# A cross-attention and FFN kernel: VectorE's second router placed ahead of a running sum and a pair of reductions, and the guard of the router's sum written to PSUM

## The reference

```python
h = norm(q) ; ig, fg = gates(h, ctx, ctx)
csum = cumsum(log_sigmoid(fg))               # running sum over the tokens, per head
log_D = csum_i - csum_j + ig_j  (j <= i) ;  D = exp(log_D - max_j log_D)
C = (q k^T / 8 + q . rpe[hops]) * D
x = x + headnorm((C / (max(|sum C|, exp(-max)) + 1e-6)) @ v)

xf = norm(x) ; probs = softmax(xf @ gate_w.T)        # 8 experts + 2 null
weights, selected = top_k(probs, 2)
tw = weights * (selected < 8)
denom = tw.sum() ; denom = where(denom > 0, denom, 1)
out = x + base(xf) + base_b + 2 * sum_e (tw/denom)_e * B_e (A_e xf)
```

## Time and profile before

| | |
|---|---|
| median of 3 runs | 3359.31 us (3355.43 to 3362.64) |
| the profiled execution's own time | 3363.58 us |
| its span, first to last instruction | 3361.5 us |
| PE busy | 2958.6 us (88%) |
| DVE busy | 2447.4 us (73%) |
| POOL busy | 2006.5 us (60%) |
| ACT busy | 1944.9 us (58%) |
| first `gate_stats` of a full round, and the last | 1463.69 and 3243.66 us, 29 rounds apart |

### The profile page before, as it was taken

The page is one execution under the profiler, slowest core; times in us unless marked ns, Lnnn a source line. Parts: engine busy times, 40 slices in busy tenths (PEclk is TensorE's granted clock), DMA queues, the critical chain, the costliest instruction groups (busy, mean ns, idle before and its releaser), DMA issues.

```text
span 3361.5 us, 69962 instructions
## 1 busy us (share of the span) xinstructions
PE 2958.6 (88%) x24660; PEld 1856.5 (55%) x24660; DVE 2447.4 (73%) x5100; ACT 1944.9 (58%) x4654; POOL 2006.5 (60%) x2195
## 2 busy tenths in 40 slices
PE   6778777787777776799999999999999999999997
PEld 4555455454444444465666566656656566566564
DVE  5655555555555555688888888888888888888875
ACT  3444444444444443576666666766666667667663
POOL 6777777777777775254454554544545545545453
PEclk8888889989999999799999999999999999999999
DMA  8999999999999998665565565655655555556551
GB/s 277 346 346 350 320 350 347 341 349 345 348 342 349 347 348 303 183 184 174 166 186 174 173 186 177 182 177 167 185 171 175 182 179 172 178 171 188 173 149 58
DMA packets 413325, 799.98 MB, mean 238 GB/s; under 512 B 107290, under 2 KB 211738, under 8 KB 410932
## 3 DMA queue, kind: packets, MB, share of 16 engines
q1 hardware_dynamic: 311988, 453.61, 43.0%
q0 software_dynamic: 82560, 270.60, 24.0%
q10 hardware_dynamic: 18432, 71.31, 5.5%
HBM read 618.02 MB, written 176.69 MB: 236 GB/s over the span
## 4 chain that ended last, share of the span: by engine, by line
PE 36%; POOL 21%; DMA 14%; issue 14%; DVE 11%; ACT 3%; SPq 0%; POOLq 0%; DVEq 0%; ACTq 0%
DMA arena<-in_L_xattn_rpe_dram,arena 14%; PE psum L1752 8%; POOL arena L784 7%; PE psum L1580 6%; PE psum L1596 4%; PE psum L1669 3%; PE psum L1704 3%; PE psum L1681 3%; POOL arena L827 3%; PE psum L1607 3%; PE psum L1756 2%; POOL arena L817 2%; POOL arena L822 2%; POOL arena L838 2%; POOL arena L771 2%
## 5 line engine op out<-in xcount | busy, mean ns | idle before, releaser
L784 POOL DMA_INDIRECT arena<-in_L_xattn_rpe_dram,arena x768 | 734.0, 956 | 239.5 <-issue 182.4
L1580 PE MATMUL psum<-arena 128*128 128x128 f32 x4128 | 615.4, 297 | 194.5 <-DMA arena<-in_L_xattn_rpe_dram,arena 183.1
L1580 PEld LDWEIGHTS psum<-arena 128*128 128x128 f32 x4128 | 488.7, 151 | 430.6 <-DMA arena<-in_L_xattn_rpe_dram,arena 299.6
L981 ACT ACTIVATE arena<-arena 128x512 f32<-128x512 f32 (+3 forms) x1024 | 496.4, 555 | 42.1 <-PE psum L1704 39.2
L1752 PE MATMUL psum<-arena 128*128 128x512 f32 x1024 | 496.5, 597 | 6.1 <-DVE arena L1377 5.9
L1327 DVE TENSOR_TENSOR arena<-psum,arena 128x1024 f32<-128x1024 f32 (+1 forms) x384 | 386.9, 1043 | 135.7 <-PE psum L1681 126.4
L809 POOL TENSOR_SCALAR_AFFINE_SELECT arena<-arena 128x256 f32<-128x256 f32 x256 | 129.7, 507 | 525.7 <-ACT arena L981 524.7
L563 DVE COPY arena<-psum 128x512 f32<-128x512 f32 x384 | 263.7, 689 | 245.8 <-PE psum L1580 242.2
L572 DVE COPY arena<-psum 128x416 f32<-128x416 f32 (+15 forms) x512 | 225.2, 442 | 278.6 <-PE psum L1596 272.5
L1596 PE MATMUL psum<-arena 64*32 64x416 f32 (+7 forms) x8192 | 364.1, 424 | 57.3 <-ACT arena L895 36.8
L563 ACT COPY arena<-psum 128x512 f32<-128x512 f32 x384 | 225.8, 588 | 257.0 <-PE psum L1580 254.5
(11 more groups left out here) (112 smaller groups left out, 4643.0 us busy)
## 6 DMA issues: line engine op xcount, KB each, us to landing
arena<-in_x_dram SPq DMA_DIRECT2D x256, 256.0 KB, 4.3
arena<-gate_rows SPq DMA_DIRECT2D x128, 512.0 KB, 4.4
arena<-in_x_dram SPq DMA_DIRECT2D x512, 64.0 KB
arena<-in_ctx_dram SPq DMA_DIRECT2D x32, 1024.0 KB, 6.6
out_dram<-arena SPq DMA_DIRECT2D x128, 256.0 KB, 2.1
arena<-in_L_xattn_rpe_dram,arena POOLq DMA_INDIRECT x1032
arena<-hop_products SPq DMA_DIRECT2D x128, 128.0 KB, 2.6
arena<-hop_products SPq DMA_DIRECT2D x128, 120.0 KB, 2.5
```

What stands on the lines that cost most here:

```text
L784: nc.gpsimd.indirect_dma_start(out=rows[set_of(n, v)][:, t, :], out_offset=None, in_=rpe[:, :], in_offset=bass.IndirectOffsetOnAxis(ap=her ...
L981: last = nc.scalar.activation(decay[u % DECAYS][:, e, at:at + width], top_pair[p % 2][:, e * S + j * P:e * S + j * P + width], ACT.Exp, bi ...
L1580: last = nc.tensor.transpose(turn_bank(o)[:, q * P:(q + 1) * P], own[:, q * P:(q + 1) * P], ident)
```

## The change

Two things. First, in the FFN's tiles 0 and 1 three steps of DVE are put in another order. Before: `two_weights(3)`, `layer(rf, 2)`, `gates_2`, `pair_sums(ra, 1)`, `output(rf, 0)`, `router(rf, 1)`, `two_weights(4)`. Now: `two_weights(3)`, `output(rf, 0)`, `layer(rf, 2)`, `router(rf, 1)`, `gates_2`, `pair_sums(ra, 1)`, `two_weights(4)`. Second, the guard in all four routers becomes a `tensor_scalar`, whose one tensor is `den` and whose second scalar is the same column, and its result goes to a column of PSUM bank 7 that nothing else uses, so the reciprocal reads PSUM.

```diff
+    def Z_GUARD(z):
+        return z[:, ER + E_ALL + E:ER + E_ALL + E + 1]
...
         for d in range(1, DOUBLES + 1):
             part = d // DOUBLES
-            if 3 <= d:
+            if 3 <= d and d != 4:
                 dve_f_steps[part] += [(n, d - 3) for n in ROUTER]
             if d < 3:
                 dve_f_steps[part] += [(n, d - 1) for n in LAYER]
             if d == 3:
-                dve_f_steps[part] += [(n, 2) for n in LAYER]
-            if 3 <= d:
+                dve_f_steps[part] += [("out", 0)] + [(n, 2) for n in LAYER] + [(n, 1) for n in ROUTER]
+            if 4 <= d:
                 dve_f_steps[part].append(("out", d - 3))
...
-                    gap, den, dz, rd = (route[:, c:c + 1] for c in range(2, 6))
+                    gap, den, rd = (route[:, c:c + 1] for c in range(2, 5))
+                    dz = Z_GUARD(bank(7))
...
-                    nc.vector.scalar_tensor_tensor(dz, den, 0.0, den, ALU.is_le, ALU.add).then_inc(*dve_f.inc(("guard", t)))
+                    nc.vector.tensor_scalar(dz, den, 0.0, den, ALU.is_le, ALU.add).then_inc(*dve_f.inc(("guard", t)))
...
                 if ra:
                     two_weights(3)
                 if rf:
+                    output(rf, 0)
                     layer(rf, 2)
+                    router(rf, 1)
                 if rp:
                     gates_2()
                 if ra:
                     pair_sums(ra, 1)
-                if rf:
-                    output(rf, 0)
-
-                if rf:
-                    router(rf, 1)
+
                 if ra:
                     two_weights(4)
```

## The result

The changed kernel took 3315.59 us (median of 4 runs, 3314.29 to 3316.65) against 3358.32 us of the kernel before; the ratio is 0.9864, with a 95% interval of 0.9837 to 0.9892. A second set of runs of the same kernel gave 0.9879 (0.9862 to 0.9896). The profiled execution took 3316.65 us, its span is 3314.6 us. Against the profiled execution of before that is 46.9 us less; the forecast was 36.6. The median is inside the range given, near its low end of 3314; the ratio of the paired runs, times 3359.31 us, is 3313.6, just under it. So the gain was larger than forecast. Three executions in a slower state (5747 us of the kernel before, 4648 of "output 0 behind", 4778 of "router 1 behind, early load") are left out of every median and ratio here.

What follows compares the result with a forecast made beforehand. Bound: per round, the longer of PE's 60.05 us and the DMA-started DVE chain. 34.2 (rounds) + 2.8 (end) - 0.4 (last routers) = 36.6 us off 3363.58 gives 3327.0; runs' median 4.3 lower, so 3323, range 3314 to 3342.

Steps and rivals of the forecast that it cites:

- What bounds the kernel: Second-stage rounds: the longer of PE's own 60.05 us and residual DMA plus DVE stretch, awaited at `mix` and `gate_stats`.
- The guard: All routers: new guard takes 0.22 us, saving 0.92 in router 0 and 1.05 in router 1; PSUM reciprocal costs nothing extra.
- Ahead of layer 2: Router 0 ends 0.92 us earlier; output 0 runs 2001.95 to 2002.60, starting layer 2 0.1 us late in the followed round.
- Behind layer 2: DVE from layer 2's start to L1317's end: 12.50 us falls to 10.85, plus the running sum's hold.
- The hold w of the running sum: Running sum on DVE held by a POOL product: 0.4 us, bounds 0 and 1.27.
- X + 15.24 + w: Round by the chain, X being L822's start after `gate_stats`: 59.85 us at mean X 44.2, 60.75 at the latest.
- signs of being wrong: Running sum at 2.4 us, L1308 still 1.68, guards near 1.1, or `x_res` landing later than 45 us into the round.
- PE's own 60.05 us: PE's time per second-stage round, the floor, from a 60.35 us round with PE busy for 60.02.
- forecast of 34.2 us: Gain in the 29 full rounds: mean round 61.38 to 60.2 us, 1.18 us each.
- the 38.6 us: Most the change could take from the 29 rounds: PE's waiting of 1.33 us a round.
- The end: Last attention round: output 0 no longer queues behind layer 2, gaining 2.8 us (bounds 0 and 3); last routers return 0.4.
- The rival with the scan held for a whole instruction: Running sum held 1.27 us in nearly every round: 60.7 on average, 3338 us in all; chance 0.2.

Runs made afterwards that it cites:

- output 0 behind: Changed kernel with output 0 put back behind the pair's sums: 3408.8 us, ratio 1.0177 to the kernel before.
- router 1 behind, early load: Changed kernel with router 1 put back behind the running sum and pair's sums, and residual tile 2's load moved up: 3310.4 us, ratio 0.9860.
- Experiments 7: Kernel before with only residual tile 2's load moved ahead of the sixteen hop loads of pair 3: 3326.5 us, ratio 0.9901.
- experiment 8: Changed kernel with residual tile 2's load moved ahead of the sixteen hop loads of pair 3: 3312.8 us, ratio 0.9863.
- experiments 5: Changed kernel with the one-tensor guard's result in the old SBUF column instead of PSUM: 3317.1 us, ratio 0.9878.
- 6: Changed kernel with the guard of two SBUF tensors as before, its result in PSUM: 3338.8 us, ratio 0.9941.
- 2: Changed kernel with the old guard, two SBUF tensors and SBUF result, so the new order alone: 3338.8 us, ratio 0.9946.
- the control: Changed kernel run once more, unchanged (the second set): 3319.8 us, ratio 0.9879, mean round 60.10 us.
- experiment 4: Changed kernel with router 1 put back behind the running sum and pair's sums, output 0 still ahead: 3327.1 us, ratio 0.9910.

## Why the prediction was right in kind, and the step that failed

**What bounds the kernel: right.** Two places of waiting on PE, one unbroken DVE stretch, and the DMA of residual tile 2 as its start. Experiments 7 and 8 show that start directly.

**The guard: right.** Taken as 0.22 us, measured 0.222; the reciprocal from PSUM costs 5 ns more. That two SBUF tensors are what is held is shown by experiments 5 and 6 with the router's last step. The reason that I gave for PSUM, from the section "Why PSUM operands drop a tier" of the Trainium skill's "VectorE: DVE Perf Modes", made no difference here: with the result in SBUF the guard took 216 ns at most.

**Ahead of layer 2: right.** Output 0 was put at 2001.95 to 2002.60, 47.0 us into the round, and starts at 46.96; layer 2 was put at the later of that and POOL.

**Behind layer 2: right in kind, the parts off by tenths.** The hold w of the running sum was taken as 0.4 us and is 0.58 in the median (1.77 - 1.19); L1312 isn't held. For the latest round the sum X + 15.24 + w with the measured terms gives 45.9 + 15.24 + 0.58 = 61.7 us, measured 61.53, so the rest of the chain is 0.2 us shorter than I put it (15.05). That w was too small by as much as the rest was too large is luck. Of the signs of being wrong one came true: `x_res` landed later than 45 us in four rounds (45.35 to 45.9), which are four of the five long ones. And the running sum, at 2.17 us at most, went above the 1.2 to 1.6 that I had given.

**PE's own 60.05 us: this is the step that failed.** I took it from a round of 60.35 us in which PE is busy for 60.02. PE takes 59.88. It waited longer than the profile showed, at two places. PE of the kernel before, in that round:

```profile
2123.87 1.21 PE L1733 MATMUL psum<-arena 128*128 128x138 f32 x8
2125.02 1.94 PE L1704 MATMUL psum<-arena 128*64 128x512 f32 x12
...
2135.63 1.51 PE L1704 MATMUL psum<-arena 128*64 128x256 f32 x8
2137.44 0.35 PE L1654 MATMUL psum<-arena 40*128 40x40 f32 x3 [0.30 <-ACT arena L1064]
```

and of the changed kernel, in the round to 2119.31:

```profile
2106.20 1.11 PE L1736 MATMUL psum<-arena 128*128 128x138 f32 x8
2107.23 1.94 PE L1707 MATMUL psum<-arena 128*64 128x512 f32 x12
...
2117.85 1.51 PE L1707 MATMUL psum<-arena 128*64 128x256 f32 x8
2119.31 0.36 PE L1657 MATMUL psum<-arena 40*128 40x40 f32 x3
```

Ahead of `gate_stats` it is 1.81 us from start to start with a wait shown as 0.30, and 1.46 us with none, so the wait was 0.35. And `routes(1)` (L1733) is shown busy for 1.21 us before and 1.11 now, 1.15 and 1.03 us from start to start: a wait of 0.12 us within it, counted as busy. Its input is ACT's L1037, which stood behind L1048 and so behind `gates_1` and router 0's held guard. The other runs bear this out: in the four kernels in which that guard is held (before, 2, 6 and 7) `routes(1)` takes 1.14 us from start to start in the median, in the ten other traces 1.04, whatever the order. Together they are the 0.47 us between 60.35 and 59.88. This 0.17 us a round is 4.9 us in 29 rounds. It lifts the forecast of 34.2 us to 39.1; the measured 37.1 lies 2 below that, since w and the late DMAs (X up to 45.9, not 45.1) kept five rounds long. It also made the lower end of the range too high: with 59.88 it is 3309 and not 3314. And the 38.6 us that I had called the most that could be had from these rounds is 29 x (61.38 - 59.88) = 43.5; experiment 8 takes 1779.97 - 1736.90 = 43.1.

**The end: right in kind, its size partly luck.** Output 0 no longer waits behind layer 2, and PE stands 1.11 us before L1720 for `mix` instead. Forecast was 2.8 less 0.4, and this trace has 2.4 us. But the trace of the second set ends 117.1 us behind its last `gate_stats` and has only 0.7: there L826 of that round started 44.6 us behind it, here 43.7, before 44.3. So the size follows a DMA that scatters by more than half of the term.

**What was not in the sum.** The 7.5 us ahead of the first full round. Of these 1.2 are the round before it (55.62 to 54.43 us), which has the same stretch and which I left out; the other 6.3 lie before any code that differs, and the control shows that they scatter. Taken out, the profiles give 37.1 + 2.4 + 1.2 = 40.7 us, and the two ratios give 45.7 (0.9864) and 40.6 (0.9879) of 3359.31 us. Against the forecast 36.6 the 40.7 are 2.9 more in the rounds and 1.2 ahead of them; the further 5.0 us of the first ratio lie, as far as the profiled pair shows, ahead of any code that differs, and the second ratio doesn't have them.

The rival with the scan held for a whole instruction was wrong in its price too: even a hold of 0.93 us, in the common round above, stays under PE's own time when the DMA is early.

## What to carry to other kernels

When a stretch of one engine is waited for at two places, ask first what starts it and what lies in it that could be held: here a DMA issued behind sixteen others and a one-column instruction with two SBUF tensors, and each partly hid the other. Moving a step ahead is worth only as much as the step that frees the bank it needs moves with it; the router ahead of an unmoved output cost 1.4 to 2.1%. And take an engine's own time from a stretch in which it waits for nothing, from start to start, not from a stretch with a wait less the idle time shown.

## What the runs showed of the hardware

A hold works both ways and for one instruction at a time: POOL's L831 took 1.96 us instead of 1.04 beside the running sum, and an instruction of 128x1 on DVE was held for up to 1.1 us. When two POOL products follow each other at once, a waiting DVE instruction mostly missed the gap between them before the change (router 1's guard: 1.28 us in 19 of 29 rounds, 0.16 in the other ten, its start 0 to 6 ns ahead of POOL's next product in both), and where it did get in, the next one with two SBUF tensors was held in its stead. Where the starts lay further apart, the one that started first went first: in experiment 4 the running sum took 1.2 to 1.4 us when it started 37 ns or more ahead of L821, which then took 2.2, and 2.0 to 2.3 when it started 45 to 370 ns behind it. One column from one SBUF tensor isn't held, wherever it is written (216 and 223 ns at most), while eight columns from SBUF to SBUF took up to 596 ns. Why the two differ wasn't tried.
